# Group norm and a shifted 3x3 smoothing: ScalarE's order by pairs of units, and SyncE's loads and stores by kind of unit

## Chip, cores and metric

One core of a Trainium2 chip runs the kernel. The metric is the device time of one execution in microseconds; the time given for a kernel is the median of its runs.

## What is computed

The input x has 16 images of 768 channels with 64 x 64 pixels, in f32. There are 48 positions of 16 channels each, and every position has an offset: a multiple of 16 pixels between -48 and 48 in each direction, plus a small random part. The reference does this:

```python
kern = jnp.exp(-(kx * kx + ky * ky) / (2.0 * SIGMA * SIGMA))
kern = kern / kern.sum(axis=(1, 2), keepdims=True)
kern_c = jnp.repeat(kern, bind, axis=0)
out = lax.conv_general_dilated(shifted, kern_c[:, None, :, :], window_strides=(1, 1), padding='SAME', feature_group_count=C, dimension_numbers=('NCHW', 'OIHW', 'NCHW'))
...
m = jnp.mean(g, axis=(2, 3, 4), keepdims=True)
s = jnp.var(g, axis=(2, 3, 4), keepdims=True)
return ((g - m) / jnp.sqrt(s + eps)).reshape(v.shape)
...
x = x + _L0_conv_ref(_gn(x), L0_conv_offset)
```

So every channel is normalised over its group of 24 channels, shifted by whole pixels with zeros moved in, smoothed with a separable 3 x 3 kernel, and added to x. Where a shift is large, only a part of the picture gets anything added.

## The kernel before

**Tiles and units.** A tile is one position for 8 images: 128 partitions (channel and image) by 4096 pixels in f32, 2 MB. There are 96 tiles, and each is loaded once into one of nine slots of `xs` (slot n % 9), changed in place and stored from there. Three neighbouring tiles (48 channels, two groups of the norm) are a unit; there are 32 units. `PAIRS` and `ORDER` (lines 45 and 46) set the order of units: they come in pairs, the even unit of a pair with positions near the centre (small shifts, large windows to change; called large here), the odd one with positions far from it (small). So tiles 6k to 6k+2 are large, and 6k+3 to 6k+5 small.

**Engines.** Each engine has its own program, and they meet by semaphores.

- SyncE (lines 166 to 187) issues all DMAs. After nine loads it goes through the tiles: the store of tile n, which waits for VectorE's `tile_done`, then the load of tile n+8, which waits until the store of tile n-1 has landed. All go through one hardware queue, in the order of issue.
- TensorE (lines 230 to 284) sums a tile over channels and images of a group by 8 matmuls of 512 columns (each of them two rows of the trace), into one bank `sum_ps` for the three tiles of a unit. In the time of unit u it does: the sums of the first two tiles of u+1, the variances of u (which need the squares of u), the sums of the third tile of u+1, and the means of u+1.
- ScalarE (lines 286 to 390) does for each tile two things. `square` (line 349) sums the squares of a tile around the mean, 4096 elements. `fill_frame` copies the rows of the tile that are used, less the mean, into `frame` (line 316), a picture with a margin of zeros, and then clears one column of it (line 323, the edge). The copy is chosen by a branch out of four heights, and its place comes from a table word in `fills`, read into a register by `load_fill` (line 297). The copy waits until VectorE has smoothed the tile before out of the one `frame`. Besides, per unit: `sum_means` (line 333), `means` (338), `means_to_fill` (342) and `variances` (357).
- VectorE (lines 392 to 553) builds the tables at the start, then loops over the tiles. Of a tile it does five operations: two smooth a row from `frame` into `smooth` (lines 506 and 511), the first of which waits for the edge; three add the result to the tile (lines 515, 518 and 521), the first of which waits for GpSimd's weights. The sizes are chosen by four branches over 16 kinds of window, of which kind 0 is the full picture.
- GpSimd (lines 189 to 228) turns the variances of a unit into weights, by ten small operations.

**ScalarE's order in a unit u**, which the change alters, is the same for all units (`unit_of`, line 360); in short:

```python
fill_frame(u, 0); next_fill(u, 0); variances(u, first)
sum_means(u + 1)
fill_frame(u, 1); next_fill(u, 1)
means(u + 1); square(u + 1, 0)
fill_frame(u, 2); next_fill(u, 2)
means_to_fill(u + 1); square(u + 1, 1); square(u + 1, 2)
```

`next_fill` reads the next table word, after the edge. Unit 0 and the last unit stand outside the loop of units 1 to 30.

## Time and profile before

| | |
|---|---|
| median of 3 runs | 1102.96 us (1101.12 to 1103.66) |
| the profiled execution | 1103.31 us |
| its span, first to last instruction | 1101.1 us |
| TensorE matmul busy | 831.8 us (76%) |
| VectorE busy | 835.1 us (76%) |
| ScalarE busy | 660.6 us (60%) |
| GpSimd busy | 375.1 us (34%) |
| DMA moved | 403.08 MB, mean 366 GB/s |

The span is a little shorter than the time of the same execution, which also holds what lies around it. Busy shares are means over the whole span; matmul ends are modelled, so TensorE's share is no measure of its peak. In rows, PE is TensorE, DVE is VectorE, ACT is ScalarE, POOL is GpSimd, SP is SyncE, and a q behind a name is the engine's instruction queue. L316 is line 316 of the kernel. Register and branch instructions don't count as busy.

### The profile page before, as it was taken

How to read it: one execution, taken by the hardware profiler on the slowest of the kernel's cores; microseconds unless marked ns; L12 is line 12 of the kernel's file. 1: busy time of each engine (PE TensorE's matmuls, PEld its weight loads, DVE VectorE, ACT ScalarE, POOL GpSimd, SP SyncE). 2: the span in 40 equal slices, each digit the busy share in tenths (PEclk: the TensorE clock that was granted, in tenths of full speed). 3: DMA queues.
4: the chain of work that ended last, by engine and by line, in shares of the span. 5: the costliest groups of instructions: out<-in, count | busy, mean ns of one | idle time of the engine just before them, and what ended most of it. 6: DMA issues, size and time to landing. Idle time of an engine off the chain costs nothing.

```text
span 1101.1 us, 9789 instructions
## 1 busy us (share of the span) xinstructions
PE 831.8 (76%) x2176; PEld 398.2 (36%) x2176; DVE 835.1 (76%) x566; ACT 660.6 (60%) x547; POOL 375.1 (34%) x332
## 2 busy tenths in 40 slices
PE   6976976788787798769848887788898787788810
PEld 2432433333343343324424443343344343343310
DVE  8198696976958768696784979788788849659685
ACT  0564546556477574766556666666566574767771
POOL 3123332536321323242732334342325317223212
PEclk9998998989799899889869999998988899788955
DMA  9737979899899798989799999999999996998937
GB/s 372 316 144 273 428 310 397 356 375 387 332 400 432 296 429 328 410 329 402 332 347 430 405 405 427 417 430 407 432 410 427 352 430 265 402 427 343 382 156 301
DMA packets 27819, 403.08 MB, mean 366 GB/s; under 512 B 3216, under 2 KB 3216, under 8 KB 3216
## 3 DMA queue, kind: packets, MB, share of 16 engines
q1 hardware_dynamic: 27792, 402.71, 89.1%
q8 instruction: 17, 0.28, 0.1%
q14 instruction: 10, 0.08, 0.0%
HBM read 201.38 MB, written 201.33 MB: 366 GB/s over the span
## 4 chain that ended last, share of the span: by engine, by line
DVE 41%; PE 16%; DMA 14%; issue 10%; ACT 8%; POOL 5%; ACTq 3%; DVEq 2%; SPq 0%; POOLq 0%
PE sum_ps L246 15%; DMA xs<-x_dram 11%; DVE xs L515 9%; DVE xs L518 9%; DVE smooth L511 8%; DVE smooth L506 7%; DVE xs L521 7%; ACT frame L316 6%; DMA out_dram<-xs 3%; POOL small L212 2%; POOL small L216 2%; ACT unused L349 1%; ACTq L297 1%; ACTq L316 1%; DVEq L506 1%
## 5 line engine op out<-in xcount | busy, mean ns | idle before, releaser
L246 PE MATMUL sum_ps<-xs,bands 128*128 128x512 f32 x1024 | 500.2, 645 | 27.8 <-DMA xs<-x_dram 27.8
L349 ACT ACTIVATE unused<-xs,small 128x4096 bf16 (+1 forms) x96 | 356.1, 3709 | 20.7 <-ACT small L342 7.6
L506 DVE SCALAR_TENSOR_TENSOR smooth<-frame,xs 128x1700 f32 (+5 forms) x96 | 163.6, 1704 | 213.0 <-ACT frame L323 167.9
L246 PE MATMUL sum_ps<-xs,halves 128*128 128x512 f32 x512 | 251.2, 648 | 73.5 <-DMA xs<-x_dram 73.5
L246 PEld LDWEIGHTS sum_ps<-xs,bands 128*128 128x128 f32 x1024 | 207.4, 208 | 271.5 <-issue 265.9
L316 ACT ACTIVATE frame<-xs,small (+1 forms) x96 | 223.3, 2326 | 111.9 <-DVE smooth L511 109.6
L212 POOL TENSOR_TENSOR small<-small 128x3 f32<-128x3 f32 x32 | 56.2, 1755 | 682.9 <-ACT small L357 682.9
L515 DVE SCALAR_TENSOR_TENSOR xs<-smooth,small,xs 128x1700 f32 (+5 forms) x96 | 163.6, 1704 | 26.0 <-POOL small L224 23.4
L246 PEld LDWEIGHTS sum_ps<-xs,halves 128*128 128x128 f32 x512 | 104.0, 208 | 219.5 <-issue 125.2
L511 DVE SCALAR_TENSOR_TENSOR smooth<-frame,xs,smooth 128x1700 f32<-128x1700 f32 (+5 forms) x96 | 163.6, 1704 | 9.7 <-DVE smooth L506 5.5
L518 DVE SCALAR_TENSOR_TENSOR xs<-smooth,small,xs 128x594 f32 (+9 forms) x96 | 159.8, 1665 | 3.4
L521 DVE SCALAR_TENSOR_TENSOR xs<-smooth,small,xs 128x594 f32 (+9 forms) x96 | 159.8, 1664 | 3.4
L333 ACT ACTIVATE sum_ps<-sum_ps 128x512 f32<-128x512 f32 x32 | 18.6, 582 | 201.3 <-PE sum_ps L246 201.3
L216 POOL TENSOR_SCALAR small<-small 128x1 f32<-128x1 f32 x96 | 129.0, 1344 | 3.3
L224 POOL TENSOR_SCALAR small<-base_w,small 128x3 f32<-128x3 f32 x96 | 104.1, 1085 | 9.5
L219 POOL TENSOR_SCALAR small<-small 128x1 f32<-128x1 f32 x96 | 78.5, 817 | 8.4
L268 PE MATMUL var_ps<-small,halves 128*128 128x1 f32 x64 | 12.8, 270 | 52.5 <-ACT unused L349 52.4
L272 PE MATMUL var_ps<-small,bands 128*128 128x1 f32 x64 | 14.6, 298 | 47.4 <-ACT unused L349 47.4
L323 ACT ACTIVATE frame<-small 128x64 f32 x96 | 31.4, 327 | 19.0 <-ACT frame L316 19.0
L256 PE MATMUL mean_ps<-small,halves 128*128 128x1 f32 x64 | 12.2, 260 | 24.9 <-ACT sum_ps L333 24.9
L268 PEld LDWEIGHTS var_ps<-small,halves 128*128 128x128 f32 x64 | 10.7, 209 | 53.5 <-ACT unused L349 53.5
L272 PEld LDWEIGHTS var_ps<-small,bands 128*128 128x128 f32 x64 | 12.2, 239 | 49.1 <-ACT unused L349 49.1
(80 smaller groups left out, 259.6 us busy)
## 6 DMA issues: line engine op xcount, KB each, us to landing
xs<-x_dram SPq DMA_DIRECT2D x96, 2048.0 KB, 14.7
out_dram<-xs SPq DMA_DIRECT2D x96, 2048.0 KB, 12.1
smooth<-offset_dram SPq DMA_DIRECT2D x1, 48.0 KB, 4.1
```

Of the source, the lines that this page charges most:

```text
L212: V.tensor_tensor(rstd0, var, power, ALU.pow).then_inc(rstd_step, 1)
L216: V.tensor_scalar(fix[:, column], var[:, column], rstd0[:, column], rstd0[:, column], ALU.mult, ALU.mult).then_inc(rstd_step, 1)
L219: V.tensor_scalar(rstd[:, column], fix[:, column], -0.5, 1.5, ALU.mult, ALU.add).then_inc(rstd_step, 1)
L224: V.tensor_scalar(col_w[:, now * UT + i, :], base_w[:, u * UT + i, :], rstd0[:, column], rstd[:, column], ALU.mult, ALU.mult).then_inc(col ...
L246: last = nc.tensor.matmul(sum_ps[:, :], (FIRST, SAME, SECOND)[i], slot_px(n, c * BANK, (c + 1) * BANK), start=(i == 0 and c == 0), stop=(i ...
L316: nc.scalar.activation(frame[:, bass.ds(b, rows * PITCH)].rearrange("p (r c) -> p r c", c=PITCH)[:, :, LEFT:LEFT + W], xs[:, bass.ds(a, ro ...
L349: nc.scalar.activation(unused[:, :], xs[:, bass.ds(n % SLOTS * PIX, PIX)], ACT.Square, bias=neg_mean[:, i:i + 1], accum_out=squares[:, i:i ...
L506: V.scalar_tensor_tensor(sm, frame_window(-1), side_w[:, bass.ds(n, 1), 0], frame_window(0), ALU.mult, ALU.add).wait_op(frame_ready, done_ ...
L511: V.scalar_tensor_tensor(sm, frame_window(1), side_w[:, bass.ds(n, 1), 1], sm, ALU.mult, ALU.add).wait_op(half_smooth, done_count, "sem-ge ...
L515: V.scalar_tensor_tensor(x_window(0, rows), sm, col_flat[:, bass.ds(weights + 1, 1)], x_window(0, rows), ALU.mult, ALU.add).wait_op(smooth ...
L518: V.scalar_tensor_tensor(x_window(1, rows), sm[:, 0:rows - 1], col_flat[:, bass.ds(weights, 1)], x_window(1, rows), ALU.mult, ALU.add).wai ...
L521: V.scalar_tensor_tensor(x_window(0, rows - 1), sm[:, 1:rows], col_flat[:, bass.ds(weights + 2, 1)], x_window(0, rows - 1), ALU.mult, ALU. ...
```

## The change

**SyncE.** After the store of tile n, no load, one or two loads follow, by n % 6. With b the first tile of a pair: store b, store b+1, loads b+9 and b+10, store b+2, store b+3, load b+11, store b+4, load b+12, store b+5, loads b+13 and b+14. Each load waits for the store of the tile nine before it, as before. So load b+10 now stands ahead of store b+2 and load b+14 ahead of store b+6; both wait for the store issued just before them.

```diff
+            AGAIN = [(), (0, 1), (), (2,), (3,), (4, 5)]
             for n in range(TILES):
                 store(n)
-                if 1 <= n <= TILES - SLOTS:
-                    load(n - 1 + SLOTS)
+                for i in AGAIN[n % len(AGAIN)]:
+                    m = n - n % len(AGAIN) + i + SLOTS
+                    if m < TILES:
+                        load(m)
```

**ScalarE.** The table word of the next tile is read behind the copy and ahead of the wait for its end; its column is first put into a register of its own, for the edge. Large and small units get orders of their own, and the loop goes over pairs of units.

```diff
-            def fill_frame(u, i):
+            def fill_frame(u, i, last=False):
...
-                column = (word & (1 << EDGE_BITS) - 1).with_bounds(min_val=LEFT - 1, max_val=PITCH - 1)
+                act.reg_mov(column, word & (1 << EDGE_BITS) - 1)
+                edge = act.snap(column, min_val=LEFT - 1, max_val=PITCH - 1)
...
                 choose(act, rows_kind, 0, len(SIDES), emit)
+                if not last:
+                    load_fill(u * UT + i + 1)
+                    act.reg_mov(slot, (base + PIX) % (SLOTS * PIX))
                 act.wait_ge(frame_copied, act.snap(u * UT + i + 1))
...
-            def unit_of(u, ahead=True, first=False):
+            def unit_of(u, large, ahead=True, first=False):
 
                 fill_frame(u, 0)
-                next_fill(u, 0)
                 variances(u, first)
-                if ahead:
+                if large:
+
+                    fill_frame(u, 1)
                     sum_means(u + 1)
-                fill_frame(u, 1)
-                next_fill(u, 1)
-                if ahead:
                     means(u + 1)
                     square(u + 1, 0)
-                fill_frame(u, 2)
+                    square(u + 1, 1)
+                elif ahead:
+                    sum_means(u + 1)
+                    means(u + 1)
+                    square(u + 1, 0)
+                    fill_frame(u, 1)
+                    square(u + 1, 1)
+                else:
+                    fill_frame(u, 1)
+                fill_frame(u, 2, last=not ahead)
                 if ahead:
-                    next_fill(u, 2)
                     means_to_fill(u + 1)
-                    square(u + 1, 1)
                     square(u + 1, 2)
...
-            unit_of(0, first=True)
+            unit_of(0, large=True, first=True)
             act.addr_align(256, max_nops=0)
-            with act.Fori(1, UNITS - 1) as u:
-                unit_of(u)
-            unit_of(UNITS - 1, ahead=False)
+            with act.Fori(0, UNITS // 2 - 1) as pair:
+                unit_of(act.snap(2 * pair + 1), large=False)
+                unit_of(act.snap(2 * pair + 2), large=True)
+            unit_of(UNITS - 1, large=False, ahead=False)
```

**VectorE.** The kinds of window are numbered from the other end, so that kind 0 is now the smallest window. At the start, one operation more works out the number.

```diff
-            V.scalar_tensor_tensor(parts[:, KIND], kind[:, :, 1], float(len(SIDES)), kind[:, :, 0], ALU.mult, ALU.add)
+
+            chained(V.scalar_tensor_tensor(edge[:, :, 0], kind[:, :, 1], float(len(SIDES)), kind[:, :, 0],
+                                           ALU.mult, ALU.add))
+            V.tensor_scalar(parts[:, KIND], edge[:, :, 0], -1.0, float(len(SIDES) ** 2 - 1), ALU.mult, ALU.add)
...
-                    ky, kx = divmod(code, len(SIDES))
+                    ky, kx = divmod(len(SIDES) ** 2 - 1 - code, len(SIDES))
```

**The order of instructions at two places.** First, ScalarE in the loop, where it has cleared the edge of a unit's first frame; in these rows ISA and REGISTER_ALU are register work. Before, in every unit:

```order
L323 ACTIVATE frame<-small 128x64
L297 ISA
L297 TENSOR_LOAD fills
L329 ISA
L357 ACTIVATE small<-var_ps,small 128x3
L332 REGISTER_ALU
L333 ACTIVATE sum_ps,small<-sum_ps 128x512
L301 ISA
L161 COMPARE_AND_BRANCH x2
```

And now, in the small unit:

```order
L304 TENSOR_LOAD fills
L334 ISA
L336 ISA
L336 ACTIVATE frame<-small 128x64
L363 REGISTER_ALU
L366 ACTIVATE small<-var_ps,small 128x3
L341 REGISTER_ALU
L342 ACTIVATE sum_ps,small<-sum_ps 128x512
L347 ACTIVATE small<-mean_ps 128x3
L357 REGISTER_ALU
L358 ISA
L358 ACTIVATE unused,small<-xs,small 128x4096
```

The table word (TENSOR_LOAD) has moved ahead of the edge. Behind the scaling of the sums, where the branches of the second frame's copy came, the means and the first square of the next unit follow now. ScalarE's loop has 122 instructions before, for one unit, and 234 now, for two; VectorE's has 246.

Second, SyncE at the start. Before:

```order
L173 DMA xs<-x_dram 128x4096 x9
L178 DMA out_dram<-xs 128x4096 x2
L173 DMA xs<-x_dram 128x4096
L178 DMA out_dram<-xs 128x4096
L173 DMA xs<-x_dram 128x4096
```

And now:

```order
L173 DMA xs<-x_dram 128x4096 x9
L178 DMA out_dram<-xs 128x4096 x2
L173 DMA xs<-x_dram 128x4096 x2
L178 DMA out_dram<-xs 128x4096 x2
L173 DMA xs<-x_dram 128x4096
```

The load of tile 10 has moved ahead of the store of tile 2; no DMA is added or taken away.

## Rows read from the trace of the kernel before

**Rows 1.** Page of the profile: the DMA queues, their packets, MB and share.
```profile
q1 hardware_dynamic: 27792, 402.71, 89.1%
q8 instruction: 17, 0.28, 0.1%
q14 instruction: 10, 0.08, 0.0%
```

**Rows 2.** Windows: one row per stretch, with the columns named in the first row.
```profile
core 0: us, PE busy (x) PEld busy (x) DVE busy (x) ACT busy (x) POOL busy (x), PEclk, DMA share, GB/s
50.90:118.60 67.70, 51.81 (x124) 24.11 (x124) 54.16 (x30) 40.25 (x35) 21.57 (x20) 0.85 0.57 223
118.60:326.20 207.60, 159.15 (x426) 76.44 (x425) 162.46 (x91) 120.76 (x102) 79.27 (x60) 0.90 0.91 370
326.20:598.50 272.30, 210.09 (x545) 100.96 (x544) 204.42 (x121) 173.90 (x136) 93.06 (x80) 0.87 0.91 373
598.50:836.90 238.40, 199.87 (x529) 93.72 (x528) 195.37 (x121) 150.65 (x136) 84.69 (x80) 0.94 1.00 417
836.90:1038.40 201.50, 162.09 (x428) 78.76 (x427) 147.27 (x91) 129.94 (x102) 70.77 (x60) 0.87 0.92 377
1038.40:1101.10 62.70, 9.44 (x33) 5.90 (x31) 46.63 (x30) 27.66 (x22) 17.26 (x20) 0.57 0.57 243
```

**Rows 3.** Waits: who waited for whom; total us, times, longest us.
```profile
DVE smooth L506 <- ACT frame L323: 167.9, 42, 23.0
...
DVE xs L515 <- POOL small L224: 23.4, 20, 2.1
...
ACT small L338 <- issue: 18.1, 31, 1.4
```

**Rows 4.** Timeline, VectorE: start us, us, operation; in brackets the wait before it.
```profile
118.62 1.99 DVE L506 SCALAR_TENSOR_TENSOR smooth<-frame,xs 128x1700 f32 x1 [5.38 <-ACT frame L323]
...
169.09 0.86 DVE L506 SCALAR_TENSOR_TENSOR smooth<-frame,xs 128x612 f32 x1 [1.92 <-issue]
...
178.30 1.16 DVE L515 SCALAR_TENSOR_TENSOR xs<-smooth,small,xs 128x900 f32 x1
...
180.63 1.10 DVE L521 SCALAR_TENSOR_TENSOR xs<-smooth,small,xs 128x850 f32 x1
187.10 3.55 DVE L506 SCALAR_TENSOR_TENSOR smooth<-frame,xs 128x3200 f32 x1 [5.37 <-ACT frame L323]
...
875.05 1.42 DVE L506 SCALAR_TENSOR_TENSOR smooth<-frame,xs 128x1156 f32 x1 [2.41 <-ACT frame L323]
...
895.70 1.16 DVE L506 SCALAR_TENSOR_TENSOR smooth<-frame,xs 128x900 f32 x1 [3.88 <-ACT frame L323]
...
987.63 1.99 DVE L506 SCALAR_TENSOR_TENSOR smooth<-frame,xs 128x1700 f32 x1 [4.11 <-ACT frame L323]
...
1038.36 1.16 DVE L506 SCALAR_TENSOR_TENSOR smooth<-frame,xs 128x900 f32 x1 [4.83 <-ACT frame L323]
```

**Rows 5.** Timeline, ScalarE, from 165 to 189 us.
```profile
165.87 1.27 ACT L316 ACTIVATE frame<-xs,small  x1 [7.64 <-DVE smooth L511]
...
175.89 3.71 ACT L349 ACTIVATE unused<-xs,small 128x4096 bf16 x1 [0.26 <-ACT small L342]
...
183.57 2.97 ACT L316 ACTIVATE frame<-xs,small  x1
...
188.86 0.26 ACT L357 ACTIVATE small<-var_ps,small 128x3 f32<-128x3 f32 x1 [1.79 <-PE var_ps L273]
```

**Rows 6.** Timeline, TensorE: the sums of tile 16.
```profile
177.30 10.07 PE L246 MATMUL sum_ps<-xs,halves 128*128 128x512 f32 x16 [9.58 <-DMA xs<-x_dram]
```

**Rows 7.** Timeline, SyncE: the store of tile 7 and the load of tile 16.
```profile
145.95 0.33 SPq L178 DMA_DIRECT2D out_dram<-xs  x1
...
164.38 0.43 SPq L173 DMA_DIRECT2D xs<-x_dram  x1
```

**Rows 8.** Page of the profile: DMA issues, KB each, median us to landing.
```profile
smooth<-offset_dram SPq DMA_DIRECT2D x1, 48.0 KB, 4.1
```

More of the change, by code:

```diff
@@ L294, in _ @@
             slot = act.alloc_register("slot")
+            column = act.alloc_register("column")
             def load_fill(n):
                 act.reg_load(entry, fills[0:1, bass.ds(n, 1)])
-            def fill_frame(u, i):
+            def fill_frame(u, i, last=False):
                 word = act.snap(entry, min_val=0, max_val=(len(SIDES) << EDGE_BITS + ROW_BITS) - 1)
-                column = (word & (1 << EDGE_BITS) - 1).with_bounds(min_val=LEFT - 1, max_val=PITCH - 1)
+                act.reg_mov(column, word & (1 << EDGE_BITS) - 1)
+                edge = act.snap(column, min_val=LEFT - 1, max_val=PITCH - 1)
                 row = (word >> EDGE_BITS) & (1 << ROW_BITS) - 1
                 rows_kind = act.snap(word >> EDGE_BITS + ROW_BITS)
-                source = act.snap(act.snap(slot, min_val=0, max_val=(SLOTS - 1) * PIX) + row * W)
+                base = act.snap(slot, min_val=0, max_val=(SLOTS - 1) * PIX)
+                source = act.snap(base + row * W)
                 target = act.snap(row * PITCH + PAD * PITCH)
@@ L321, in fill_frame @@
                 choose(act, rows_kind, 0, len(SIDES), emit)
+                if not last:
+                    load_fill(u * UT + i + 1)
+                    act.reg_mov(slot, (base + PIX) % (SLOTS * PIX))
                 act.wait_ge(frame_copied, act.snap(u * UT + i + 1))
-                nc.scalar.activation(frame_v[:, PAD:PAD + H, bass.ds(column, 1)],
+                nc.scalar.activation(frame_v[:, PAD:PAD + H, bass.ds(edge, 1)],
                                      zeros.unsqueeze(1).to_broadcast([P, H, 1]),
                                      ACT.Copy).then_inc(frame_ready, 1)
-            def next_fill(u, i):
-                load_fill(u * UT + i + 1)
-                act.reg_mov(slot, act.snap(act.snap(slot, min_val=0, max_val=(SLOTS - 1) * PIX) + PIX) % (SLOTS * PIX))
             def sum_means(u):
```

## The prediction

> **What bounds the kernel now.** I read the windows first, then the waits, then single rows. The first two say that two things take turns. From 598.5 to 836.9 us, four pairs of units, the DMA engines are busy all the time at 417 GB/s: 59.6 us for a pair, which is 12 transfers of 2 MB [rows 2]. That is the floor of a pair. The pairs before and behind it take longer: three in 207.6 us, four in 272.3 and three in 201.5, so 69.2, 68.1 and 67.2 each [rows 2]. There the DMA share is 0.91 to 0.92, and VectorE, with 54.2, 51.1 and 49.1 us a pair, isn't full either. Over the whole span the queue is busy 89.1% [rows 1].
>
> Who makes these pairs long is seen at VectorE, which runs the tiles in order. Its first operation of a tile waited for ScalarE's frame 42 times, 167.9 us in all [rows 3]; 23.0 of it is the start. Most of the rest falls on one place: the first large tile of a pair, behind a small unit. Twelve of these waits stand outside the full-DMA stretch, from 5.38 us at 118.6 to 4.83 at 1038.4, together 77.5 us [rows 4]. A gap between small tiles that nobody causes but VectorE's own register work is 1.92 us [rows 4]. So ScalarE costs on average 4.5 us (77.5 / 12, less 1.9) at each of the twelve.
>
> Why ScalarE is late there, in the pair that starts at 118.6: in the small unit it sat idle 7.64 us ahead of the copy at 165.87, with the next unit's sums already scaled; then, behind the last small copy, it did two squares (the first at 175.89), and only at 183.57 the first large frame, though tile 11 had been smoothed by 178.3 (its third operation starts then; all [rows 4, 5]). VectorE ended tile 11 at 181.73 and started tile 12 at 187.10.
>
> A second chain is as long. The variance of the next unit is computed behind the sums of two more tiles on TensorE. The last of these, 177.30 to 187.4, had waited 9.58 us for a load [rows 6]. That load (tile 16) was issued at 164.38, because it stood behind the store of tile 8, a tile of five operations of 3.5 us, though its own slot's store, of tile 7, had been issued at 145.95 [rows 7]. ScalarE's variance came only at 188.86 [rows 5].
>
> **The change, part by part.**
>
> *ScalarE, small unit.* The means and the first square move ahead of the second copy, the second square ahead of the third; one square stays behind it. Nothing is added. In the pair above: square 1 runs from 159.4 to 163.2, inside the idle 7.64; the copy at 165.87 stays where it is; square 2 ends by 171.5, the third copy by 173.3, square 3 by 177.5, and the large copy starts when tile 11 is smoothed, at 178.3, and is through (2.97 and 0.33 with their waits, 3.5) at 181.8. VectorE is then bound by itself: 181.73 and 1.9 make 183.6, against 187.10. At all twelve places: 77.5 less 12 times 1.9 is **54.7 us**. Bounds: nothing, if the late sums or loads put the wait elsewhere, and 54.7.
>
> *ScalarE, large unit.* The second copy moves ahead of the sums. Before, it had to wait for TensorE to finish a unit whose last load came late: VectorE waited for the second large tile in five places, up to 4.11 us (at 987.63), 10.8 us in all [rows 4]. About 1.0 of each is VectorE's own: **5.5 us** won (0 to 10.8). The first two squares now stand ahead of the third copy; its deadline is the end of the second large tile, and the squares end some 18 us after the pair's start, against 23 or more for that deadline, so they cost nothing. That cover is gone only where the two first large tiles take under 18 us together.
>
> *What is given back.* The third copy, a square (3.71), the variance, the sums of one tile (up to 10.07 [rows 6]), the scaling and means (2.3) and a square (3.71) now stand in one chain ahead of the second small copy: 25 us with that copy's own wait. VectorE has in this time the rest of the second large tile, the third, and the first small one. Where the third large tile takes 5 x 1.16 and the first small one 5 x 1.42 us [rows 4], that is some 22 to 24 us, and the chain comes 1 to 3 us late; four pairs are of this kind or near it. I take back **7 us**, between 0 and 16 (4 pairs, 4 us each).
>
> *Early table words.* The table word is read while the copy runs, and not between the frame's edge and the next operation. What shows of it is "issue": 18.1 us at 31 means, 0.58 each [rows 3]. Most lies where ScalarE has idle time. The gain at the twelve places is inside the 54.7 already, as the bound there is VectorE's 1.9. The variance is taken some 0.5 us earlier; but the 20 waits for GpSimd's weights (23.4 us, 1.17 each [rows 3]) stay, because GpSimd's operations end only when VectorE's do. Nothing; at most half of them, 12.
>
> *SyncE.* In a pair of tiles b to b+5 the loads of b+10 and b+14 now go ahead of the stores of b+2 and b+6. Each then waits for a store that was issued just before it. Another load (b+9, b+13) is queued between, about 5 us of work at 2 MB and 417 GB/s, and a store alone lands in 6 to 7, so the queue runs nearly dry but not long. Queued behind the waiting load are the stores of a large tile that isn't finished (b+2), or of b+6, which can be held back some 6 us where the first large tile is short; the DMA engines work meanwhile. For tile 16 the issue moves from 164.38 to about 153.5, so its sums end near 174, and the variance isn't held up. This gives no term of its own: it lets the 54.7 stand. It also fills idle DMA time while the third large tile is computed.
>
> *VectorE.* The table's kinds are numbered the other way round, so that small tiles come first in the branches. One setup operation more (about 0.2 us, beside loads). The own gap of 1.92 may move by 0.2 either way in 48 small tiles: zero, bounds 10 us each way.
>
> **Sum.** 1103.3 us of the profiled execution, less 54.7, less 5.5, plus 7, is 1050.1. The median of the runs is 0.3 lower, so **1050 us**. Check against the floors: the ten long pairs take 681.4 us now (207.6, 272.3 and 201.5). For the three with 54.2 us of VectorE work its own floor is about 62 (three gaps of 1.92 and three short ones, 7 in all, and one weight wait of 1.17), for the seven others the DMA floor is 59.6: 604 in all. The forecast leaves them some 633, between the two.
>
> **Rivals.**
>
> *Both floors are reached.* If the giving back doesn't happen and the small branches help, the ten pairs take 604, 77 less, and start and end some 6 less: 1020 to 1030. For it: nothing in the trace holds ScalarE up when it isn't in the wrong order. Against: the chain of 25 us.
>
> *DMA is the bound earlier.* With fewer holes the queue must be full nearly always. If reads and writes in the new order get 390 GB/s, a pair (25.17 MB) takes 64.5 us and sixteen take 1032. The windows of start and end hold 29 and 27 us of idle DMA time (0.43 of 67.7 and 62.7), of which some 46 stay: about 1078. For it: at a share of 0.91 to 0.92 there is only 8 to 9% to win. Against: 417 over 238 us [rows 2].
>
> *The loads don't come earlier.* Should the moved loads find their stores landing late, TensorE gets tile b+10 as before and the variance stays at 188.9 in the pair above. Tile 12 would reach its third operation at 190.8 (183.6 and two of 3.55), but the weights would come only as before, at some 195, and nothing is won. If that holds at seven or eight of the twelve places, 20 of the 54.7 are left: 1085.
>
> *Slower: ScalarE's loop no longer stays in its instruction memory.* Its body grows from 122 to 234 instructions, as the order of both kernels counts them, and a round has a backward branch. The place is the jump to the pair's small unit and the first frame after it; the price is at least one small transfer, 4.1 us for the offsets [rows 8], at the jump and at each of two further block edges, 12.3 a pair. The slack ahead of the small unit's first copy hides some 4 of it, and 15 rounds cost 15 x 8.3, 124 us: 1174. It decides against the change from 3.6 us exposed per round (53 / 15). Against it: VectorE's loop has 246 instructions by the same count, goes round 96 times, and the whole trace has 17 and 10 instruction packets on its two queues [rows 1]. The Trainium skill, "Runtime: NRT & Kernel Launch", section on instruction fetch mechanics, says that an engine holds a window of two pages and that a taken branch to a target outside it stalls for a fetch; by that rule with a page as long as it gives, the loop fits and the result stays 1050. This trace agrees in so far as VectorE's equally long loop shows no fetches.
>
> **How the numbers follow.** Forecast 0.60 (1036 to 1065); floors reached 0.12; DMA earlier 0.14; loads not earlier 0.09; slower 0.04; no change 0.01, if ScalarE's waits only change places. A measurement here tells 0.2% (2.2 us) from no change. Faster: 0.60 + 0.12 + 0.14 + 0.09 = 0.95; slower 0.04; within 0.2% 0.01. The range takes in the upper part of the floors' case and the DMA case: 1028 to 1080.
>
> **What would show it.** Right: first-large-tile waits at VectorE near 2 us, the sum of its waits for ScalarE's frame from 167.9 to about 90; pairs of 60 to 65 us outside the stretch 598 to 837, which stays at 59.6; the load of tile 16 issued some 10 us before store 8; DMA share 0.93 to 0.94 over the span; variance within 1 us of the first large frame. Wrong: waits of 3 us or more ahead of the second small tile, TensorE waiting 9 us for tile b+10 still, or instruction packets beyond the 27 of before by one or two per round.

## The result, and the profile after

The changed kernel takes **1061.55 us** (median of 4 runs, 1056.45 to 1063.07) against 1102.04 before (4 runs). The ratio is 0.963, with a 95% interval of 0.9587 to 0.9673: 40.5 us less, where 53 were forecast. The direction and the range (1028 to 1080) hold. The profiled execution took 1056.45 us, its span 1054.2, which is 46.9 less than the span before. All rows of after come from it; it is the fastest of the four runs, so spans compared below show some 6 us more than the medians do.

First the page's queue rows, as [rows 1]:

```profile
q1 hardware_dynamic: 27792, 402.71, 93.2%
q8 instruction: 17, 0.28, 0.1%
q14 instruction: 11, 0.09, 0.0%
```

The queue is busy 93.2% of a shorter span, as the forecast said (0.93 to 0.94). The instruction packets are 28 instead of 27, so ScalarE's doubled loop is not fetched anew.

The windows, cut at the same places of the program as [rows 2] (the starts of the same pairs):

```profile
core 0: us, PE busy (x) PEld busy (x) DVE busy (x) ACT busy (x) POOL busy (x), PEclk, DMA share, GB/s
50.10:112.70 62.60, 49.33 (x137) 24.16 (x136) 54.16 (x30) 39.49 (x35) 23.12 (x21) 0.92 0.62 244
112.70:300.50 187.80, 153.69 (x392) 72.05 (x393) 162.49 (x91) 118.47 (x101) 86.82 (x59) 0.88 0.96 393
300.50:557.50 257.00, 213.41 (x562) 102.64 (x560) 204.41 (x120) 170.80 (x137) 101.15 (x80) 0.88 0.97 397
557.50:804.10 246.60, 206.47 (x544) 97.87 (x544) 195.40 (x120) 147.83 (x137) 79.28 (x82) 0.90 1.00 410
804.10:989.20 185.10, 153.06 (x408) 72.52 (x408) 147.23 (x90) 127.73 (x102) 77.33 (x61) 0.92 1.00 410
989.20:1054.20 65.00, 13.07 (x36) 7.56 (x36) 46.67 (x30) 27.14 (x21) 17.22 (x19) 0.59 0.58 248
```

The three pairs of the second row take 187.8 us, against 207.6; the four of the third 257.0 against 272.3; the last three 185.1 against 201.5. But the four pairs that had been full of DMA before now take **246.6 us, against 238.4**, and their rate has gone from 417 to 410 GB/s. The share is 1.00 not in four pairs, but in seven, and 0.96 to 0.97 in the seven ahead of them.

The waits, as [rows 3]:

```profile
PE sum_ps L252 <- DMA xs<-x_dram: 121.1, 40, 10.7
DVE smooth L524 <- ACT frame L336: 115.2, 31, 21.6
...
DVE xs L533 <- POOL small L230: 16.6, 20, 2.6
```

VectorE's waits for ScalarE's frame went from 167.9 to 115.2 us (21.6 of it the start), its waits for weights from 23.4 to 16.6. TensorE now waits 121.1 us for loads. Before, it was

```profile
PE sum_ps L246 <- DMA xs<-x_dram: 101.3, 39, 10.7
```

For the place that the forecast worked out, here is VectorE, with the end of tile 11 and the start of tile 12, as [rows 4]. The last row, from further on, is the start of tile 26, a third large tile:

```profile
169.90 1.16 DVE L533 SCALAR_TENSOR_TENSOR xs<-smooth,small,xs 128x900 f32 x1
...
172.23 1.10 DVE L539 SCALAR_TENSOR_TENSOR xs<-smooth,small,xs 128x850 f32 x1
174.98 3.58 DVE L524 SCALAR_TENSOR_TENSOR smooth<-frame,xs 128x3200 f32 x1 [1.64 <-issue]
...
329.64 3.55 DVE L524 SCALAR_TENSOR_TENSOR smooth<-frame,xs 128x3200 f32 x1 [5.66 <-ACT frame L336]
```

The wait ahead of tile 12 is 1.64 us, VectorE's own register work, where it had been 5.37. ScalarE beside it, as [rows 5]:

```profile
151.40 3.71 ACT L358 ACTIVATE unused<-xs,small 128x4096 bf16 x1 [0.25 <-ACT small L347]
...
158.13 1.27 ACT L326 ACTIVATE frame<-xs,small  x1 [2.93 <-DVE smooth L529]
159.52 0.33 ACT L336 ACTIVATE frame<-small 128x64 f32 x1
159.75 3.71 ACT L358 ACTIVATE unused<-xs,small 128x4096 bf16 x1
...
163.80 1.26 ACT L326 ACTIVATE frame<-xs,small  x1 [0.24 <-issue]
...
165.34 0.19 ACT L351 ACTIVATE small<-small 128x3 f32<-128x3 f32 x1
165.78 3.71 ACT L358 ACTIVATE unused<-xs,small 128x4096 bf16 x1 [0.25 <-ACT small L351]
...
170.30 2.99 ACT L326 ACTIVATE frame<-xs,small  x1 [0.72 <-DVE smooth L529]
173.42 0.33 ACT L336 ACTIVATE frame<-small 128x64 f32 x1
173.58 0.25 ACT L366 ACTIVATE small<-var_ps,small 128x3 f32<-128x3 f32 x1
```

This is the forecast's order of events: the first square (151.40), the second copy, the second square (159.75), the third copy, one square (165.78), and then the large copy, which waits 0.72 us for VectorE and for nothing else. The variance follows at 173.58, right behind the edge, where it had come 1.8 us behind it. TensorE had summed tile 16 by then, and SyncE had issued its load at 147, the second of a merged row with tile 15's (as [rows 6, 7]):

```profile
158.99 7.03 PE L252 MATMUL sum_ps<-xs,halves 128*128 128x512 f32 x16
```

```profile
142.10 5.21 SPq L173 DMA_DIRECT2D xs<-x_dram  x2
156.28 3.52 SPq L178 DMA_DIRECT2D out_dram<-xs  x2
```

The same sums took 10.07 us before and 7.03 now. That difference isn't the order's: the granted clock was 0.71 in the window of the old row (177.3 to 187.4) and 1.00 in that of the new one (159.0 to 166.1).

At tile 26 the picture is another. ScalarE ahead of it:

```profile
315.69 0.58 ACT L342 ACTIVATE sum_ps<-sum_ps 128x512 f32<-128x512 f32 x1 [7.39 <-PE sum_ps L252]
...
317.73 3.71 ACT L358 ACTIVATE unused<-xs,small 128x4096 bf16 x1 [0.25 <-ACT small L347]
...
321.70 3.71 ACT L358 ACTIVATE unused<-xs,small 128x4096 bf16 x1 [0.17 <-ACT unused L358]
...
325.41 3.74 ACT L326 ACTIVATE frame<-xs,small 128x4096 f32 x1
```

The third large tile's copy starts at 325.41 right behind two squares, and these stand behind the scaling of the sums at 315.69. VectorE had ended tile 25 at 324.0 and waits 5.66 us. The sums themselves took 9.40 us there, at a granted clock of 0.76, where the next tile's took 7.11 at 1.00; so some 2.3 of the 5.66 us are TensorE's clock, an estimate from these two.

Where all of VectorE's gaps lie is best seen by a table. It adds, over the 16 pairs, VectorE's idle time ahead of the first operation of a tile, by the tile's place in its pair, from the timeline (without the start of tile 0); the last column is the weight wait from the waits view. e1 to e12 are the runs of the next section. e3 reorders nothing, so its row shows what two profiles of the same work can differ by: nearly 4 us in a column.

| kernel | 1st large | 2nd large | 3rd large | 1st small | 2nd small | 3rd small | weights |
|---|---|---|---|---|---|---|---|
| before | 89.0 | 17.0 | 6.2 | 13.4 | 31.3 | 32.4 | 23.4 |
| after | 28.3 | 11.2 | 27.1 | 9.6 | 50.6 | 25.8 | 16.6 |
| e1, SyncE alone | 94.0 | 26.0 | 6.2 | 13.4 | 31.6 | 33.0 | 21.3 |
| e2, SyncE as before | 29.5 | 11.2 | 10.0 | 9.6 | 49.6 | 26.4 | 34.1 |
| e3, loop alone | 90.0 | 20.7 | 6.2 | 13.2 | 31.5 | 32.7 | 22.2 |
| e4, words late | 38.5 | 11.4 | 22.1 | 9.6 | 49.8 | 30.3 | 21.0 |
| e5, only b+10 early | 27.6 | 11.3 | 28.1 | 9.6 | 51.8 | 25.9 | 14.4 |
| e6, only b+14 early | 26.3 | 11.4 | 13.3 | 9.6 | 46.8 | 26.5 | 35.3 |
| e7, large: square late | 30.6 | 11.4 | 11.3 | 11.1 | 71.8 | 25.9 | 20.9 |
| e8, small: copy early | 33.4 | 11.3 | 30.4 | 9.6 | 21.7 | 57.1 | 21.5 |
| e9, half squares | 25.3 | 11.3 | 18.8 | 9.6 | 39.5 | 24.3 | 31.2 |
| e10, half stores | 26.9 | 11.3 | 8.4 | 9.6 | 29.2 | 26.4 | 12.0 |
| e11, kinds as before | 26.2 | 10.1 | 29.2 | 11.6 | 52.1 | 29.1 | 15.3 |
| e12, b+11 early too | 30.7 | 11.2 | 15.6 | 9.6 | 72.7 | 25.8 | 26.9 |

From before to after, the first column gives 60.7 us, the second 5.8, the two with smaller changes 3.8 and 6.6, the weights 6.8: 83.7 won. The third large and second small tiles take 20.9 and 19.3 of it back. That leaves 43.5 of the 46.9 us by which the span is shorter; 1.1 us more is the earlier start of tile 0 (50.1 against 51.2), and the small rest I haven't traced.

### The profile page after: what moved, and what is told of

It is laid out like the page before. It is cut to its first block, busy times and chain, and to the rows that moved or that the text cites. A ratio compares the mean times of both kernels' runs of the same rounds, so it can differ in the third digit from the quotient of the medians.

```text
span 1054.2 us, 9775 instructions
## 1 busy us (share of the span) xinstructions
PE 827.6 (79%) x2176; PEld 395.0 (37%) x2176; DVE 835.4 (79%) x567; ACT 649.1 (62%) x547; POOL 393.3 (37%) x332
## 3 DMA queue, kind: packets, MB, share of 16 engines
q1 hardware_dynamic: 27792, 402.71, 93.2%
## 4 chain that ended last, share of the span: by engine, by line
DVE 32%; DMA 25%; PE 17%; issue 7%; ACT 7%; POOL 6%; DVEq 3%; ACTq 2%; SPq 0%; POOLq 0%
DMA out_dram<-xs 16%; PE sum_ps L252 16%; DMA xs<-x_dram 10%; DVE xs L533 7%; DVE xs L536 7%; DVE smooth L529 6%; DVE xs L539 6%; DVE smooth L524 5%; ACT frame L326 5%; POOL small L218 2%; POOL small L222 2%; POOL small L225 1%; POOL small L230 1%; ACT sum_ps L342 1%; ACTq L304 1%
## 5 line engine op out<-in xcount | busy, mean ns | idle before, releaser
L252 PE MATMUL sum_ps<-xs,bands 128*128 128x512 f32 x1024 | 524.7, 671 | 101.5 <-DMA xs<-x_dram 101.5
L358 ACT ACTIVATE unused<-xs,small 128x4096 bf16 (+1 forms) x96 | 356.1, 3709 | 17.9 <-ACT small L347 7.6
L252 PEld LDWEIGHTS sum_ps<-xs,bands 128*128 128x128 f32 x1024 | 216.0, 217 | 361.3 <-issue 303.4
L524 DVE SCALAR_TENSOR_TENSOR smooth<-frame,xs 128x1700 f32 (+5 forms) x96 | 163.7, 1705 | 174.0 <-ACT frame L336 115.2
L252 PE MATMUL sum_ps<-xs,halves 128*128 128x512 f32 x512 | 232.7, 608 | 19.5 <-DMA xs<-x_dram 19.5
L533 DVE SCALAR_TENSOR_TENSOR xs<-smooth,small,xs 128x1700 f32 (+5 forms) x96 | 163.6, 1704 | 19.3 <-POOL small L230 16.6
L252 PEld LDWEIGHTS sum_ps<-xs,halves 128*128 128x128 f32 x512 | 98.8, 195 | 150.0 <-issue 120.9
L222 POOL TENSOR_SCALAR small<-small 128x1 f32<-128x1 f32 x96 | 124.0, 1292 | 3.3
L230 POOL TENSOR_SCALAR small<-base_w,small 128x3 f32<-128x3 f32 x96 | 112.9, 1176 | 9.5
L225 POOL TENSOR_SCALAR small<-small 128x1 f32<-128x1 f32 x96 | 94.2, 981 | 8.4
L262 PEld LDWEIGHTS mean_ps<-small,halves 128*128 128x128 f32 x64 | 9.9, 195 | 62.8 <-ACT sum_ps L342 62.8
L278 PE MATMUL var_ps<-small,bands 128*128 128x1 f32 x64 | 12.4, 263 | 24.9 <-ACT unused L358 24.9
L347 ACT ACTIVATE small<-mean_ps 128x3 f32<-128x3 f32 x32 | 5.6, 175 | 30.6 <-PE mean_ps L264 30.6
L278 PEld LDWEIGHTS var_ps<-small,bands 128*128 128x128 f32 x64 | 10.3, 202 | 25.8 <-ACT unused L358 25.8
```

The lines of the kernel that those rows point to most:

```text
L222: V.tensor_scalar(fix[:, column], var[:, column], rstd0[:, column], rstd0[:, column], ALU.mult, ALU.mult).then_inc(rstd_step, 1)
L225: V.tensor_scalar(rstd[:, column], fix[:, column], -0.5, 1.5, ALU.mult, ALU.add).then_inc(rstd_step, 1)
L230: V.tensor_scalar(col_w[:, now * UT + i, :], base_w[:, u * UT + i, :], rstd0[:, column], rstd[:, column], ALU.mult, ALU.mult).then_inc(col ...
L252: last = nc.tensor.matmul(sum_ps[:, :], (FIRST, SAME, SECOND)[i], slot_px(n, c * BANK, (c + 1) * BANK), start=(i == 0 and c == 0), stop=(i ...
L358: nc.scalar.activation(unused[:, :], xs[:, bass.ds(n % SLOTS * PIX, PIX)], ACT.Square, bias=neg_mean[:, i:i + 1], accum_out=squares[:, i:i ...
L524: V.scalar_tensor_tensor(sm, frame_window(-1), side_w[:, bass.ds(n, 1), 0], frame_window(0), ALU.mult, ALU.add).wait_op(frame_ready, done_ ...
```

## The experiments

All times are medians; the ratio is to the kernel before, run on the same chip.

### e1: SyncE's order alone

The kernel before, with this of the change and no more:

```diff
+            AGAIN = [(), (0, 1), (), (2,), (3,), (4, 5)]
...
-                if 1 <= n <= TILES - SLOTS:
-                    load(n - 1 + SLOTS)
+                for i in AGAIN[n % len(AGAIN)]:
+                    m = n - n % len(AGAIN) + i + SLOTS
+                    if m < TILES:
+                        load(m)
```

> The kernel before with SyncE's new order of loads and stores and nothing else. Theory of the prediction (the order lets ScalarE's gain stand, but gives little by itself, because the first large tile of a pair still waits behind two squares): 1095 us, between 1085 and 1102. Rival (the idle DMA time was what mattered, and the new order alone fills it): 1065 to 1075, with VectorE's waits for ScalarE's frame falling from 168 to about 120 us.

Measured: 1109.96 us, ratio 1.0057 (1.0036 to 1.0078). The new order alone makes the kernel a little slower, outside both expectations. VectorE's waits, against [rows 3]:

```profile
DVE smooth L509 <- ACT frame L326: 190.2, 48, 21.9
...
DVE xs L518 <- POOL small L227: 21.3, 20, 1.1
```

They rose from 167.9 to 190.2 us. TensorE's waits for loads did fall, from 101.3 to 30.8 us, but the queue's share didn't rise (88.9% against 89.1%). So loads that come earlier are worth nothing by themselves, and their order doesn't fill the idle DMA time of before. ScalarE's orders do: in e2, below, the share rises to 92.2% with the old order of loads. The mean granted clock was lower as well (0.855 against 0.879); no run tells what that cost.

### e2: ScalarE's part alone

The changed kernel with SyncE's loop of before.

```diff
-            AGAIN = [(), (0, 1), (), (2,), (3,), (4, 5)]
...
-                for i in AGAIN[n % len(AGAIN)]:
-                    m = n - n % len(AGAIN) + i + SLOTS
-                    if m < TILES:
-                        load(m)
+                if 1 <= n <= TILES - SLOTS:
+                    load(n - 1 + SLOTS)
```

> The changed kernel with SyncE's order of before: ScalarE's orders, early table words and the numbering of kinds stay. Theory of the prediction (without the early loads the variance comes as late as before, and VectorE stalls at its third operation instead): 1080 to 1090 us, TensorE waits some 9 us for tile b+10. Rival (the first large frame is all that matters): 1060 to 1065, as the changed kernel. A third, from the trace of after (holding back the store of b+6 lengthens the stretch with full DMA from 238 to 247 us): part of the loss is made good, and the stretch from tile 48 to tile 72 is back at 238 to 240 us.

Measured: 1060.65 us, ratio 0.9628 (0.9586 to 0.967): the same as the changed kernel. The waits:

```profile
DVE smooth L521 <- ACT frame L333: 106.6, 34, 21.8
...
DVE xs L530 <- POOL small L227: 34.1, 19, 5.1
```

The theory of the prediction was half right and came to the wrong sum. The weights do come late, 34.1 us of waits against 16.6. But the third large tile waits 10.0 us, and not 27.1. What SyncE's order wins at one place it loses at the other. The store of tile 20, and behind it the load of tile 29, the last one that the squares ahead of tile 26 need, show how. In this run:

```profile
288.39 0.33 SPq L178 DMA_DIRECT2D out_dram<-xs  x1
...
297.27 0.34 SPq L173 DMA_DIRECT2D xs<-x_dram  x1
```

And in the changed kernel, where the first row is the stores of tiles 20 and 21:

```profile
280.93 6.42 SPq L178 DMA_DIRECT2D out_dram<-xs  x2
295.97 0.34 SPq L173 DMA_DIRECT2D xs<-x_dram  x1
```

Here the load is issued at 297.27, 8.9 us behind the store whose slot it takes, and the pair of tile 24 starts at 308.7. In the changed kernel two loads stand right ahead of that store, the load of tile 29 follows it by 15.0 us, and the pair starts at 300.5. The pair has moved up by 8 us, and the load by one. The granted clock was a little higher here (0.898 against 0.882); TensorE's matmuls are busy for the same time (826.8 and 827.6 us), but no run separates what the clock gave.

### e3: the longer loop alone

```diff
-            with act.Fori(1, UNITS - 1) as u:
-                unit_of(u)
+            with act.Fori(0, UNITS // 2 - 1) as pair:
+                unit_of(act.snap(2 * pair + 1))
+                unit_of(act.snap(2 * pair + 2))
```

> The kernel before with ScalarE's loop written over pairs of units, two old bodies behind each other; nothing is reordered. If the longer body stays in the instruction memory, as VectorE's loop of the same length does: 1102, within 3 us. If it has to be fetched again each round (the slower rival): 1110 to 1225 and 15 to 45 instruction packets more than 27.

Measured: 1103.88 us, ratio 0.9995 (0.9973 to 1.0017), and 28 instruction packets:

```profile
q8 instruction: 17, 0.28, 0.1%
q14 instruction: 11, 0.09, 0.0%
```

The slower rival falls: a loop of some 234 instructions costs nothing here.

### e4: table words read late

```diff
                 choose(act, rows_kind, 0, len(SIDES), emit)
-                if not last:
-                    load_fill(u * UT + i + 1)
-                    act.reg_mov(slot, (base + PIX) % (SLOTS * PIX))
                 act.wait_ge(frame_copied, act.snap(u * UT + i + 1))
...
                                      ACT.Copy).then_inc(frame_ready, 1)
+                if not last:
+                    load_fill(u * UT + i + 1)
+                    act.reg_mov(slot, (base + PIX) % (SLOTS * PIX))
```

> The changed kernel with the table words read behind the frame's edge, as before; all else as changed. By the prediction the early words give nothing, as they lie beside other work: 1061, within 4 us. Rival (ScalarE's chain is the bound now, so what stands in it counts, 0.5 us at three tiles in the ten or more pairs that it sets): 1072 to 1080.

Measured: 1069.54 us, ratio 0.9679 (0.9642 to 0.9715). That lies between the two expectations, and its interval touches that of the changed kernel, so the size isn't settled: some 5 us by the ratios, 8 by the medians. The waits that the early words remove are back:

```profile
ACT small L366 <- issue: 18.2, 27, 1.2
ACT small L351 <- issue: 18.0, 31, 1.4
ACT unused L358 <- issue: 14.1, 15, 1.1
```

They are 50.3 us together, and none of these three is in the changed kernel's list. The table shows where they count: 10.2 us at the first large tile and 4.5 at the third small one.

### e5 and e6: which of the two loads

The changed kernel with only one load moved ahead: that of b+10 in e5, that of b+14 in e6. In both the bound of a load became `SLOTS <= m < TILES`, so that the entry -1 loads nothing at the first tile.

```diff
-            AGAIN = [(), (0, 1), (), (2,), (3,), (4, 5)]
+            AGAIN = [(-1,), (0, 1), (), (2,), (3,), (4,)]
```

```diff
-            AGAIN = [(), (0, 1), (), (2,), (3,), (4, 5)]
+            AGAIN = [(), (0,), (1,), (2,), (3,), (4, 5)]
```

> The changed kernel, in which of the two loads only that of b+10 is moved ahead of a store (of b+2); the load of b+14 stands behind the store of b+6 as before. Theory formed from the runs so far (the early b+10 takes away the wait for weights at the first large tile, 32.6 to 14.5 us; the early b+14 holds back the store of b+6, so that the loads b+9 to b+11 and with them the squares come late and the third large tile waits, 10.0 to 27.1 us): both gains are had, the gaps ahead of the third large tile fall to about 10 us, the weight waits stay near 15, and the time is 1045 us, between 1040 and 1052. Rival (all of it is one DMA queue that is nearly full, and what one place wins another loses): 1058 to 1064.

> The other half: only the load of b+14 is ahead of the store of b+6. By the same theory both losses are had: weight waits at the first large tile near 32 us, gaps ahead of the third large tile near 27, 1070 to 1080 us. Rival: 1058 to 1064.

Measured: e5 1058.67 us, ratio 0.9608 (0.9576 to 0.9639); e6 1061.41, ratio 0.9627 (0.9601 to 0.9653). Neither can be told from the changed kernel or from e2. The weight waits of e5, then of e6:

```profile
DVE xs L533 <- POOL small L230: 14.4, 18, 1.1
```

```profile
DVE xs L533 <- POOL small L230: 35.3, 19, 5.8
```

Set against e2, which moves neither load, the early b+10 alone makes the whole difference of columns: it takes the weight waits from 34.1 to 14.4 and puts the third large tile's wait from 10.0 to 28.1. My theory had given the second effect to b+14, and that falls; the early b+14 alone changes no column by more than some 3 us. SyncE's rows agree: the load of tile 29 follows the store of tile 20 by 13.8 us in e5, and by 8.9 in e6 as in e2. The rival's numbers hold in both.

### e7 and e8: ScalarE's orders

e7 puts a large unit's second square behind the third copy; e8 puts a small unit's second copy ahead of means and square.

```diff
                     square(u + 1, 0)
-                    square(u + 1, 1)
                 elif ahead:
...
                     means_to_fill(u + 1)
+                    if large:
+                        square(u + 1, 1)
                     square(u + 1, 2)
```

```diff
                     sum_means(u + 1)
+                    fill_frame(u, 1)
                     means(u + 1)
                     square(u + 1, 0)
-                    fill_frame(u, 1)
                     square(u + 1, 1)
```

> The changed kernel, in which a large unit's second square stands behind the third copy again (one square ahead of it, two behind). If the squares ahead of the third copy cost what the trace of after shows (gaps of 27.1 us ahead of the third large tile, against 6.2 before), the gaps fall by some 10 us; but the variance and the sums behind it come a square (3.9 us) later, and the gaps ahead of the second small tile (50.6 us) grow by 20 to 40 us: 1070 to 1080. If TensorE's sums aren't what the second small tile waits for: 1050.

> The changed kernel, in which a small unit's second copy stands ahead of the means and the first square again, behind the scaling of the sums; both squares then run between the second and the third copy. If the square ahead of the second copy is what the 50.6 us of gaps before the second small tile cost (31.3 before), they fall to 35 or 40, but the third small tile (25.8 us of gaps) then waits for two squares, 3 us more at most of the sixteen: 1065 to 1085. If the idle time that the square fills is not needed: 1045 to 1055.

Measured: e7 1068.23 us, ratio 0.9669 (0.9631 to 0.9707); e8 1067.57, ratio 0.967 (0.9646 to 0.9695; its profiled execution was slower, at 1074.4). Both are 6 to 7 us slower by their medians, with intervals that overlap that of the changed kernel, so neither is surely slower. e7 lies just under its expected 1070 to 1080. In it the third large tile wins 15.8 us (some 10 were expected) and the second small one loses 21.2, within what was expected. In e8 the second small tile wins 28.9, more than expected, and the third loses 31.3, less than expected. Either way the wait moves; whether it grows isn't settled.

### e9 and e10: the queue or the chain

e9 squares only half of each tile (half of the sum of squares is left out). e10 stores only half of each tile (half of the output is left out).

```diff
-                nc.scalar.activation(unused[:, :], xs[:, bass.ds(n % SLOTS * PIX, PIX)], ACT.Square,
+                nc.scalar.activation(unused[:, 0:PIX // 2], xs[:, bass.ds(n % SLOTS * PIX, PIX // 2)], ACT.Square,
```

```diff
-                sp.dma_start(of_tile(out_tiles, n), slot_px(n)).then_inc(stored[n % SLOTS], 16)
+                sp.dma_start(of_tile(out_tiles, n)[:, 0:PIX // 2], slot_px(n, 0, PIX // 2)).then_inc(stored[n % SLOTS], 16)
```

> The changed kernel, in which each square of ScalarE takes only the first 2048 of a tile's 4096 elements (half of the sum of squares is left out); DMAs are as they were. Every chain of squares gets 1.85 us shorter per square, 178 us of ScalarE's work in all. If the DMA queue is the bound now (share 0.99 to 1.01 from 237 to 989 us): 1045 to 1060, and the pairs stay at 60 to 65 us. If ScalarE's chain of copies, squares and sums is the bound: the gaps ahead of the second small and the third large tile go (50.6 and 27.1 us), and the time is 1000 to 1030.

> The changed kernel, in which each store writes only the first half of a tile (half of the output is left out), so the queue has a quarter less to move; ScalarE is as it was. If the DMA queue is the bound: the pairs fall to what the engines need, 55 to 65 us by the chains of the prediction (62.8, 63.9, 60.2, 65.5, 56.6, 64.9, 57.3 by kind of pair), 1005 to 1035 in all, and the gaps ahead of the third large tile go back to 6 us. If the chain of squares and sums is the bound: 1050 to 1062 with the same gaps.

Measured: e9 **1044.76 us**, ratio 0.9466 (0.9437 to 0.9494); e10 **1013.76 us**, ratio 0.9178 (0.9157 to 0.9199). e9 is 0.2 us under its first expectation and far from its second; e10 is in its first. One window from 250 to 950 us, of before, after, e9 and e10 in this order (the columns are those of [rows 2]):

```profile
250.00:950.00 700.00, 555.78 (x1458) 266.16 (x1457) 540.43 (x318) 437.02 (x362) 256.50 (x215) 0.89 0.94 386
```

```profile
250.00:950.00 700.00, 582.70 (x1528) 276.58 (x1527) 558.48 (x337) 452.29 (x382) 264.93 (x224) 0.90 0.99 403
```

```profile
250.00:950.00 700.00, 593.20 (x1560) 281.13 (x1559) 568.90 (x342) 348.25 (x389) 249.12 (x225) 0.90 1.00 409
```

```profile
250.00:950.00 700.00, 609.12 (x1621) 294.70 (x1622) 590.50 (x358) 481.19 (x404) 290.44 (x237) 0.91 0.81 317
```

The queue's share goes from 0.94 to 0.99 with the change. Taking 164 us of squares off ScalarE (356.1 to 192.2 us busy; 178 had been expected) brings 17 us and a share of 1.00; taking a quarter off the queue brings 48 us and a share of 0.81. In e10 the third large tile's gaps are 8.4 and the second small one's 29.2, as before the change, and TensorE's waits for loads fall from 121.1 us to

```profile
PE sum_ps L252 <- DMA xs<-x_dram: 20.1, 8, 10.8
```

So the 40 us that were taken back are the queue's. Shorter squares take 19.4 us off the same two columns (e9), but 14.6 of it come back as waits for weights (16.6 to 31.2), with the queue full. The pairs of e10 from tile 6 on (62.4, 62.1, 63.5, 60.0, 59.6, 61.9, 62.4, 56.6, 55.8, 55.7, 55.9, 60.6, 63.5 and 56.3 us between their starts) are near what the engines' chains need without it. The first three of them, and the pair ahead (62.7 us), take as long as in the changed kernel (62.7, 62.2, 62.2 and 63.3 us). So the queue isn't the bound everywhere: the first four pairs are at the floor of about 62 us that the forecast worked out for VectorE, and nearly all of the 40 us lie in the pairs from tile 24 on.

### e11: VectorE's kinds as before

```diff
-                    ky, kx = divmod(len(SIDES) ** 2 - 1 - code, len(SIDES))
+                    ky, kx = divmod(code, len(SIDES))
```

and the table's kinds accordingly.

> The changed kernel with VectorE's kinds numbered as before. VectorE's own gap in front of a small tile is 0.3 to 0.5 us shorter in the trace of after (1.84 to 1.5 at the third small tile). If VectorE sets the pairs: 1068 to 1075. If the queue does, as I think now: 1061, within 4 us, and only the gaps change.

Measured: 1059.74 us, ratio 0.959 (0.9569 to 0.9612), no difference. The new numbering shortens the gaps ahead of the first small tiles by 2.0 us and of the third ones by 3.3, in all 16 pairs together; in the time none of it can be seen.

### e12: one more load early

```diff
-            AGAIN = [(), (0, 1), (), (2,), (3,), (4, 5)]
+            AGAIN = [(), (0, 1), (2,), (), (3,), (4, 5)]
```

> The changed kernel with the load of b+11 ahead of the store of b+3 as well (right behind the store of b+2). The third large tile waits for squares whose sums need tile b+11; one transfer earlier is 5 us earlier there. If that wait can be won: gaps ahead of the third large tile 27 to about 12 us, and 1050 us. If the queue is the bound, in whatever order it is filled: 1056 to 1066.

Measured: 1081.5 us, ratio 0.9805 (0.9769 to 0.9841): clearly slower than the changed kernel, which neither theory had. The third large tile did win (27.1 to 15.6 us), but the second small one waits 72.7. The window from 250 to 950:

```profile
250.00:950.00 700.00, 569.50 (x1480) 270.12 (x1478) 543.86 (x328) 440.57 (x371) 242.13 (x215) 0.88 0.95 390
```

The share is 0.95, against 0.99. The load of b+11 waits for the store just issued with nothing queued in between, and the store of b+3 stands behind it. The trace shows the queue run dry there. In the pair of tile 18 the store of tile 20 was issued at 282.07; VectorE ended tile 21 at 288.1, but its store came only at 297.64, behind the load of tile 29 at 297.27. Just before, the queue had hardly anything to move:

```profile
294.00:296.00 2.00, 2.00 (x6) 0.95 (x5) 0.58 (x2) 1.63 (x4) 0.00 (x0) 1.00 0.40 172
296.00:298.00 2.00, 2.00 (x6) 0.80 (x6) 1.88 (x4) 2.00 (x1) 0.00 (x0) 1.00 0.04 16
```

That is some 3 us idle in this pair, an estimate from the two shares. In the pairs from tile 6 on the share is 0.94 to 0.97, so by these shares the others lose about as much. No order of loads that I tried beats the changed kernel beyond the measurement's bound.

## Why the prediction was right, and where its size was off

**The first large tile: 54.7 us won.** At the twelve places that were counted, the waits fell from 77.5 to 23.7 us: 53.8. The working, with VectorE's own 1.9 us as what is left, was right to a microsecond in the sum (single waits lie between 1.12 and 4.51 us), and the events ahead of tile 12 came in the order drawn. It started at 174.98 where the sketch had 183.6; 5.9 us of this is the earlier start of its pair (112.7 against 118.6).

**The second large tile: 5.5 us.** 17.0 less 11.2 is 5.8 over all 16 pairs, and 10.8 less 6.0 is 4.8 at the five places of the forecast. Right, though e3's row (20.7) shows that this column can move by nearly 4 us between profiles of the same work.

**What is given back: 7 us.** This term failed. It was 40.2 us: 20.9 at the third large tile and 19.3 at the second small one. I had looked for it in ScalarE's chain and let the range go to 16. The half-store run shows that the chain costs next to nothing there (8.4 and 29.2 us of gaps, against 6.2 and 31.3 before). The loads come late because the queue is full. The sign that was named for being wrong came true as well: waits of 3 us or more ahead of the second small tile, in 8 of 16 pairs, up to 8.71; and the waits for ScalarE's frame fell to 115.2 us and not to about 90. The sentence "the squares end some 18 us after the pair's start, ... so they cost nothing" holds in the first pairs (from tile 6 on: the pair starts at 112.7, the squares end at 131.2), where the queue isn't the bound; at tile 26 the scaling came 15.2 us after the pair's start (315.69 less 300.5), with the squares ending 24.8 us after it.

**SyncE: no term, "it lets the 54.7 stand".** This failed as a reason, though not in the sum. Without the new order the time is the same (e2). The variance is late there, as I said, and the weights cost 17.5 us more; but that is paid for by a third large tile that doesn't wait. I had seen that each load ahead of a store delays that store, and counted it as nothing because the DMA engines work meanwhile. In a full queue the next load pays for it, since it waits for that store: 15.0 us behind it instead of 8.9 at tile 29.

**Early words: nothing (bound 12).** 5 to 8 us by e4, not settled. At the first large tile they are part of the 54.7, as was said: without them 10.2 us of it are lost. **Weights: unchanged.** They fell by 6.8 us. **Numbering: zero.** Right in time (e11), with 5.3 us of gaps for it.

**That the total came so near is in part luck.** 33 us more were given back than forecast. Against that stand some 27 us that no term had, or had smaller: 6.0 more at the first large tile (from the full-DMA stretch, which was left out), 6.8 of weights, 3.8 and 6.6 at the first and third small tiles, 1.1 at the start, and the rest that wasn't traced. By spans 46.9 us were won and 53.2 forecast; without these gains the working would have ended near 20.

**The check against the floors** was the step that should have warned me. It took the DMA floor as 59.6 us a pair, from a stretch whose rate (417 GB/s) I took for all pairs. After the change seven pairs have a share of 1.00 at 410, and the four that had been at the floor are 2 us a pair longer. So the rival "DMA is the bound earlier" came true in part: it had the right mechanism for the pairs from tile 24 on, and too high a price, 390 GB/s and 1078 us. The first four pairs stay at VectorE's floor of about 62 us, as the forecast had it.

**The rivals otherwise.** "Both floors are reached" didn't come. "The loads don't come earlier" was made real by e2: the weights were late as it said, and the time was 1060.65, not 1085, because the third large tile's wait went with it (27.1 to 10.0 us). "Slower", by the instruction memory, fell with e3: 28 packets, and 1103.88 us. The Trainium skill, "Runtime: NRT & Kernel Launch", on instruction fetch mechanics, has a taken branch stall only where its target is outside a window of two pages; no run here has a loop that would be longer than that, and these two, of 234 and 246 instructions, show no fetches.

## What to carry to other kernels

When a change takes waits out of a kernel whose DMA share is already 0.9, price it against the queue first: the stretches that are not yet full fill up, and then a part of the removed waits comes back where the next load is needed, here 40 of 84 us. Two runs tell how much: one with half of the stores (48 us here) and one with half of an engine's work (17 us). Compare them stretch by stretch, since the bound needn't be the same everywhere. In this one queue of loads and stores, once it was full, moving one load ahead of a store was a trade and no gain (e2, e5, e6). A load that waits for the store just issued, with a finished tile's store behind it, was a loss of 20 us (e12).

## What I had not expected of the hardware

The queue's rate at full share isn't one number. At a share of 1.00 it moved 417 GB/s in the four pairs of before and 410 in seven pairs of after, and single pairs at 0.99 to 1.01 lie between 406 and 424 before and between 394 and 422 after. I can't say what sets it.

The waits for GpSimd's weights fell from 23.4 to 16.6 us, though I had held them for tied to VectorE's operations. They are: in the kernel before, one and the same operation took 0.35 us while VectorE waited, and 3.59 beside a VectorE operation of 3.48 us (at 198.95):

```profile
194.84 0.35 POOL L224 TENSOR_SCALAR small<-base_w,small 128x3 f32<-128x3 f32 x1
...
199.06 3.59 POOL L224 TENSOR_SCALAR small<-base_w,small 128x3 f32<-128x3 f32 x1
```

In the changed kernel the variance at 173.58 comes ahead of VectorE's first operation on tile 12 (174.98), GpSimd's first operation starts at 173.91 in that gap and takes 0.86 us (2.17 before), and VectorE waits 0.39 us for the weights instead of 1.11. What made each of the 20 waits shorter I haven't traced.
